# Scores of two heads issued as one stage on TensorE, and new places for the last two heads' attention product

## The reference, cut to what matters

```python
q = rms_norm(x @ q_w + q_b, nq_s).reshape(B, S, H, D)
k_img = rms_norm(img_ctx @ ki_w + ki_b, nki_s).reshape(B, -1, H, D)
v_img = (img_ctx @ vi_w + vi_b).reshape(B, -1, H, D)
scores = jnp.einsum('bshd,blhd->bhsl', q, k_img) / sqrt(D)
attn = softmax(scores)
out = jnp.einsum('bhsl,blhd->bshd', attn, v_img).reshape(B, S, INNER)
return out @ o_w + o_b
```

## Time and profile before

| | us |
|---|---|
| three runs | 1355.42, 1356.98, 1357.06 |
| median | 1356.98 |
| profiled execution: its own time | 1356.92 |
| its span | 1355.1 |
| PE busy (share of span) | 1326.7 (98%) |
| PE's weight loads busy | 1155.5 (85%) |
| DVE busy | 767.6 (57%) |
| ACT busy | 765.8 (57%) |
| POOL busy | 74.1 (5%) |

### The profile page before, as it was taken

How to read it: one execution, slowest core, us unless ns; L and a number is a source line. 1 busy time by engine, 2 the same in 40 slices (tenths; PEclk the granted TensorE clock), 3 DMA queues, 4 the chain that set the end, 5 groups by cost and what they waited for, 6 DMA issues and landing times.

```text
span 1355.1 us, 26606 instructions
## 1 busy us (share of the span) xinstructions
PE 1326.7 (98%) x10367; PEld 1155.5 (85%) x10367; DVE 767.6 (57%) x2315; ACT 765.8 (57%) x2092; POOL 74.1 (5%) x114
## 2 busy tenths in 40 slices
PE   7899999999999999999999999999999999999998
PEld 6788888988898788988889888998889888888777
DVE  7644555546555464665555465564656555554575
ACT  4375666566465574756556565556646556466522
POOL 3000000010000000000000100001000000001010
PEclk9999999999999999999999999999999999999999
DMA  8312522224122321222212231122312112122100
GB/s 303 110 63 79 141 94 68 75 63 125 48 70 64 102 94 47 63 94 79 94 47 71 70 125 63 47 79 82 110 44 79 63 63 94 48 78 65 62 1 32
DMA packets 51451, 108.47 MB, mean 80 GB/s; under 512 B 8224, under 2 KB 32000, under 8 KB 50688
## 3 DMA queue, kind: packets, MB, share of 16 engines
q1 hardware_dynamic: 51328, 106.77, 24.3%
HBM read 89.98 MB, written 16.78 MB: 79 GB/s over the span
## 4 chain that ended last, share of the span: by engine, by line
PE 86%; DVE 10%; ACT 3%; issue 1%; DMA 0%; SPq 0%; DVEq 0%
PE bank L114 57%; PE bank L1053 8%; PE bank L1063 5%; PE bank L1024 3%; PE bank L1042 3%; PE bank L1163 2%; PE bank L1175 2%; PE bank L1205 1%; PE bank L1014 1%; PE bank L1117 1%; ACT xn L785 1%; PE bank L994 1%; DVE rstd L80 1%; DVE logit L1534 1%; DVE ao_lo L1525 1%
## 5 line engine op out<-in xcount | busy, mean ns | idle before, releaser
L114 PE MATMUL bank<-sv,ct_hi 128*128 128x256 f32 x1024 | 195.7, 289 | 0.0
L114 PE MATMUL bank<-so,ao_hi 128*128 128x256 f32 x1016 | 188.2, 284 | 0.3 <-DVE ao_lo L1525 0.3
L1525 DVE SCALAR_TENSOR_TENSOR ao_lo<-bank,vecs,ao_hi 128x512 fp32r<-128x512 f32 x127 | 95.3, 751 | 159.7 <-ACT ao_hi L754 158.9
L760 ACT ACTIVATE expo<-logit,least 128x64 f32<-128x64 f32 x512 | 171.6, 337 | 20.6 <-DVE least L1536 20.6
L754 ACT ACTIVATE ao_hi<-bank,vecs 128x512 fp32r<-128x512 f32 x127 | 87.0, 685 | 155.0 <-PE bank L1053 154.5
L114 PEld LDWEIGHTS bank<-so,ao_hi 128*128 128x128 f32 x1016 | 162.4, 189 | 8.5 <-issue 0.5
L114 PEld LDWEIGHTS bank<-sv,ct_hi 128*128 128x128 f32 x1024 | 156.6, 189 | 0.1
L1534 DVE TENSOR_TENSOR logit<-bank,rr 128x256 f32<-128x256 f32 x128 | 54.4, 425 | 162.4 <-PE bank L1063 161.9
L779 ACT ACTIVATE q_sb<-bank,qbias,qscale 128x512 f32<-128x512 f32 x128 | 99.3, 776 | 80.3 <-PE bank L114 79.8
L114 PE MATMUL bank<-sv,ct_lo 128*128 128x256 f32 x512 | 143.1, 279 | 0.0
L114 PE MATMUL bank<-so,ao_lo 128*128 128x256 f32 x508 | 142.3, 280 | 0.0
(11 more groups left out here) (239 smaller groups left out, 2668.0 us busy)
## 6 DMA issues: line engine op xcount, KB each, us to landing
sv<-v_scratch SPq DMA_DIRECT2D x56, 512.0 KB, 3.4
so<-o_scratch SPq DMA_DIRECT2D x56, 512.0 KB, 3.3
xin<-in_x_dram SPq DMA_DIRECT2D x8, 512.0 KB, 4.8
cin<-in_ctx_dram SPq DMA_DIRECT2D x32, 128.0 KB, 4.8
xres<-in_x_dram SPq DMA_DIRECT2D x8, 512.0 KB, 4.7
c_scratch<-cs SPq DMA_DIRECT2D x8, 512.0 KB, 5.0
v_scratch<-sv SPq DMA_DIRECT2D x8, 512.0 KB, 3.1
o_scratch<-so SPq DMA_DIRECT2D x8, 512.0 KB, 2.6
```

Of the source, the lines that this page charges most:

```text
L114: last = pe.matmul(out, lhs[a], rhs[b], start=start and n == 0, stop=stop and n == 2, **kw)
L760: last = act.activation(expo[:, t, :], logit[:, t, :], ACT.Exp, scale=-1.0, bias=least[:, t:t + 1], accum_out=rsum[:, t:t + 1])
L1525: dve.scalar_tensor_tensor(out=lo[:, :], in0=attention_bank(g, h)[:, :], scalar=vecs[:, v:v + 1], in1=hi[:, :].bitcast(F32), op0=ALU.add, ...
```

## The change

- `OUT_LAG` goes from 4 to 3, and TensorE's step gets a new order: in even steps scores(h-2) and scores(h-1) as one stage at the head of the step; then attend(h-3), share a, K(h), share b, V(h), share c, Q(h), transposes(h-2), share d, output(h-3), share e.
- `logit`, `least`, `rsum` and `q_sb` get two buffers, and the two heads' scores go to the two halves of bank `at_ps`. `expo` is gone: the exponentials are written over `logit`. `gt` now lies in `th`.
- ACT does exps(h-2) where it did exps(h-1), behind the copy of K and share b and ahead of the copy of V. The copy of Q comes ahead of `prob_copy` in odd steps and behind it in even ones.
- DVE does both heads' logits at the head of even steps, then share a, attn_lo, share b, probabilities(h-2), share c, prob_copy(h-2).
- In the tail heads 14 and 15 each have a bank and parts of their own, and the work is put in another order; the expert choice of the group before last (`expert_choice`, `expert_scale`) comes behind the last attn_lo.

```diff
@@ -103,7 +103,7 @@
-TURN_LAG, ATT_LAG, OUT_LAG = 2, 3, 4
+TURN_LAG, ATT_LAG, OUT_LAG = 2, 3, 3
...
@@ -173,8 +173,8 @@
-    least = sb("least", [P, NT])
-    rsum = sb("rsum", [P, NT])
+    least = sb("least", [P, 2, NT])
+    rsum = sb("rsum", [P, 2, NT])
...
@@ -183,9 +183,8 @@
-    q_sb = sb("q_sb", [P, GT])
-    logit = sb("logit", [P, NT, SEQ])
-    expo = sb("expo", [P, NT, SEQ])
+    q_sb = sb("q_sb", [P, 2, GT])
+    logit = sb("logit", [P, 2, NT, SEQ])
...
@@ -249,7 +248,7 @@
-    gt = sb("gt", [E1, GT])
+    gt = th[0:E1, 0, :, :].rearrange("p c d -> p (c d)")
...
@@ -462,7 +461,7 @@
-    LAST_CHOICE_AT = {"xn3": (14, "d"), ("xt3", 0): (15, "b"), ("xt3", 1): (15, "c"), "gt": (15, "e")}
+    LAST_CHOICE_AT = {"xn3": (14, "d"), ("xt3", 0): (15, "b"), ("xt3", 1): (15, "c")}
...
@@ -486,10 +485,11 @@
-        return pj_ps[0] if (g, h) == (LAST, H - 2) else pv_ps
+        return {(LAST, H - 2): pj_ps[0], (LAST, H - 1): at_ps}.get((g, h), pv_ps)
-        return [v["k"][:, 0, 0:GT] for v in (w_hi, w_lo)] if (g, h) == (LAST, H - 2) else [ao_hi, ao_lo]
+        own = g == LAST and h >= H - 2
+        return [v["k"][:, h - (H - 2), 0:GT] for v in (w_hi, w_lo)] if own else [ao_hi, ao_lo]
...
@@ -757,12 +757,14 @@
-                last = act.activation(expo[:, t, :], logit[:, t, :], ACT.Exp, scale=-1.0, bias=least[:, t:t + 1],
-                                      accum_out=rsum[:, t:t + 1])
+                last = act.activation(logit[:, h % 2, t, :], logit[:, h % 2, t, :], ACT.Exp, scale=-1.0, bias=least[:, h % 2, t:t + 1],
+                                      accum_out=rsum[:, h % 2, t:t + 1])
+            if g == LAST and h >= H - 2:
+                act.wait_ge(pv_full.sem, pv_full.count(g, h - 1))
...
@@ -776,7 +778,7 @@
-                act.activation(q_sb[:, :], bank[:, :], ACT.Identity, scale=qscale[:, h:h + 1],
+                act.activation(q_sb[:, h % 2, :], bank[:, :], ACT.Identity, scale=qscale[:, h:h + 1],
...
@@ -882,6 +884,7 @@
+            final = main and h == H - 1 and not is_body(b, NG - 1)
...
@@ -889,19 +892,22 @@
                 project(b, h, 0)
             share(b, h, "b")
             if live(b, h - TURN_LAG):
-                prob_copy(b, h - TURN_LAG)
-            share(b, h, "c")
-            if live(b, h - 1):
-                exps(b, h - 1)
+                exps(b, h - TURN_LAG)
             if main:
                 project(b, h, 1)
-                if h == H - 1 and not is_body(b, NG - 1):
+                if final:
                     split_context(b + 1)
+            share(b, h, "c")
+            soon = main and (h % 2 == 1 or (b, h) == (LAST, H - 2))
+            if soon:
+                project(b, h, 2)
+            if live(b, h - TURN_LAG):
+                prob_copy(b, h - TURN_LAG)
+            if main and not soon:
+                project(b, h, 2)
+            if final:
+                split_tokens(b + 1)
             share(b, h, "d")
-            if main:
-                project(b, h, 2)
-                if h == H - 1 and not is_body(b, NG - 1):
-                    split_tokens(b + 1)
             share(b, h, "e")
 
         def end():
...
@@ -951,13 +957,15 @@
                 step(b, h)
         for h in range(H):
             step(LAST, h)
+        exps(LAST, H - 2)
         exps(LAST, H - 1)
+        prob_copy(LAST, H - 2)
         attn_hi(LAST, H - 3)
-        prob_copy(LAST, H - 2)
+        prob_copy(LAST, H - 1)
+        attn_hi(LAST, H - 2)
+        turned_gates(NEXT)
+        attn_hi(LAST, H - 1)
         expert_exp(NEXT)
-        attn_hi(LAST, H - 2)
-        prob_copy(LAST, H - 1)
-        attn_hi(LAST, H - 1)
         end()
 
     @block.tensor
...
@@ -1035,8 +1043,10 @@
+            elif (g, h) == (LAST, H - 1):
+                l_ready.wait(pe, g, h)
-                ao_ready.wait(pe, g, h - 2 if (g, h) == (LAST, H - 1) else h - 1)
+                ao_ready.wait(pe, g, h - 1)
...
@@ -1056,12 +1066,12 @@
-            l_ready.wait(pe, g, h - 1)
+            l_ready.wait(pe, g, h - 1 if (g, h) == (LAST, H - 1) else h - 1 - h % 2)
-                    last = pe.matmul(at_ps[i * SEQ:(i + 1) * SEQ, t * SEQ:(t + 1) * SEQ],
-                                     q_sb[:, s], k_sb[:, h % 2, keys(t, i)], start=True, stop=True)
+                    last = pe.matmul(at_ps[i * SEQ:(i + 1) * SEQ, (h % 2 * NT + t) * SEQ:(h % 2 * NT + t + 1) * SEQ],
+                                     q_sb[:, h % 2, s], k_sb[:, h % 2, keys(t, i)], start=True, stop=True)
...
@@ -1287,27 +1297,33 @@
 
         def step(b, h):
             main = live(b, h)
-            if live(b, h - OUT_LAG):
-                output(b, h - OUT_LAG)
+            if (b, h) == (0, 2):
+                gr_read.wait(pe, 0, 2 * NT - 1)
+            if h % 2 == 0 and live(b, h - 2):
+                scores(b, h - 2)
+                scores(b, h - 1)
+            if (b, h) == (LAST, H - 1):
+                scores(b, h - 1)
             if live(b, h - ATT_LAG):
                 attend(b, h - ATT_LAG)
             share(b, h, "a")
             if main and (b, h) != (0, 0):
                 project(b, h, 0)
             share(b, h, "b")
+            if main:
+                values(b, h)
+            share(b, h, "c")
             if (b, h) == (0, 1):
                 norms(-1)
-                gr_read.wait(pe, 0, 2 * NT - 1)
-            if live(b, h - 1):
-                scores(b, h - 1)
+            if main:
+                project(b, h, 2)
             if live(b, h - TURN_LAG):
                 prob_transpose(b, h - TURN_LAG)
-            share(b, h, "c")
-            if main:
-                values(b, h)
             share(b, h, "d")
-            if main:
-                project(b, h, 2)
+            if live(b, h - OUT_LAG):
+                output(b, h - OUT_LAG)
+            if (b, h) == (LAST, H - 1):
+                scores(b, h)
             share(b, h, "e")
 
         def awake(bank, n):
...
@@ -1402,16 +1418,15 @@
                 step(b, h)
         for h in range(H):
             step(LAST, h)
-        scores(LAST, H - 1)
-        gate_logits(NEXT)
-        output(LAST, H - 4)
+        turned_gates(NEXT)
+        prob_transpose(LAST, H - 2)
         attend(LAST, H - 3)
-        prob_transpose(LAST, H - 2)
+        prob_transpose(LAST, H - 1)
         attend(LAST, H - 2)
-        prob_transpose(LAST, H - 1)
         output(LAST, H - 3)
         attend(LAST, H - 1)
         output(LAST, H - 2)
+        gate_logits(NEXT)
         output(LAST, H - 1)
         end()
 
...
@@ -1516,6 +1531,8 @@
+            if g == LAST and h >= H - 2:
+                dve.wait_ge(pv_full.sem, pv_full.count(g, h - 1))
...
@@ -1528,17 +1545,20 @@
-            dve.wait_ge(qk_full.sem, qk_full.count(g, h))
+            dve.wait_ge(qk_full.sem, qk_full.count(g, h if (g, h) == (LAST, H - 2) else h + 1 - h % 2))
-            chain.link(dve.tensor_tensor(logit[:, :, :], at_ps[:, 0:NT * SEQ].rearrange("p (t l) -> p t l", t=NT),
-                                         rr[:, (g - (h < 0)) % 2, :, :], ALU.mult))
-            dve.tensor_reduce(least[:, :], logit[:, :, :], AXX, ALU.min).then_inc(l_ready.sem, 1)
+            u = h % 2
+            chain.link(dve.tensor_tensor(logit[:, u, :, :], at_ps[:, u * NT * SEQ:(u + 1) * NT * SEQ].rearrange(
+                "p (t l) -> p t l", t=NT), rr[:, (g - (h < 0)) % 2, :, :], ALU.mult))
+            dve.tensor_reduce(least[:, u, :], logit[:, u, :, :], AXX, ALU.min).then_inc(l_ready.sem, 1)
-            chain.link(dve.reciprocal(rinv[:, :], rsum[:, :]))
-            dve.tensor_tensor(prob[:, :, :], expo[:, :, :], rinv[:, :].unsqueeze(2).to_broadcast([P, NT, SEQ]),
+            if (g, h) == (LAST, H - 1):
+                dve.wait_ge(pt_full.sem, pt_full.count(g, h - 1))
+            chain.link(dve.reciprocal(rinv[:, :], rsum[:, h % 2, :]))
+            dve.tensor_tensor(prob[:, :, :], logit[:, h % 2, :, :], rinv[:, :].unsqueeze(2).to_broadcast([P, NT, SEQ]),
...
@@ -1777,23 +1797,27 @@
                     late_low(LATE_AT[at])
 
         def step(b, h):
-            if h == 0 and not is_body(b, 0) and live(b, 0):
+            first = h == 0 and not is_body(b, 0) and live(b, 0)
+            if first:
                 split(b, 0)
-            if live(b, h - TURN_LAG):
-                probabilities(b, h - TURN_LAG)
-            if h == 0 and not is_body(b, 0) and live(b, 0):
-                split(b, 1)
+            if h % 2 == 0 and live(b, h - 2):
+                logits(b, h - 2)
+                logits(b, h - 1)
+            if (b, h) == (LAST, H - 1):
+                logits(b, h - 1)
             share(b, h, "a")
             if live(b, h - ATT_LAG):
                 attn_lo(b, h - ATT_LAG)
-            if is_body(b, 0) and h == 1:
+            if first:
+                split(b, 1)
+            if (b, h) == (0, 1):
                 score_factors(0)
-            if live(b, h - 1):
-                logits(b, h - 1)
+            share(b, h, "b")
+            if live(b, h - TURN_LAG):
```

(20 more changed lines are left out.)

## The result

The changed kernel takes 1361.25 us (median of 7 runs, 1361.11 to 1361.88), the kernel before 1356.96 (7 runs, 1355.33 to 1357.20): ratio 1.0036, 95% interval 1.0025 to 1.0047. It is 4.3 us slower, where 1354.0 was predicted: the sign was wrong, the range held the time. The seven runs of the kernel before lie in two groups, three at 1355.3 to 1355.5 and four at 1357.0 to 1357.2; in the later sessions, which list the clock of each run, those near 1355.5 have a mean granted clock of 0.998 or 0.999 and the longer ones 0.997. The median and the profiled execution belong to the longer ones; against the others the change loses 5.8 us.

The account below looks back on a forecast made before the run. Only TensorE's own queue, busy 98% of the span, was taken to set the end. Terms: -15 + 5.5 + 17.8 + 7.2 - 11 - 4.5 - 2.4 - 0.4 = -2.8 us from 1356.98, giving 1354 us; range 1341 to 1366.

Parts of the forecast that it names:

- Part 3: Transposes moved into the step of their own exponentials: TensorE waits for probabilities in some steps, a loss of 17.8 us.
- Part 4: DVE's probability copy queued behind step 14's score factors: attend in step 15 waits 1.2 us in six bodies, 7.2 us lost.
- Part 2: Affinities and second attention at share b no longer run into scores: 0.8 us a body, 5.5 us lost.
- Part 5: Old waits behind DVE's scale chains and the norms' sums go away: 1.4 us, a gain of 11 us over the bodies.
- Part 1: Scores in pairs enter and leave the 64-column form once, not twice: 0.23 us for each of 64, 15 us gained.
- Parts 6 and 7: Body 0's shorter stops: at the start in step 1, gain 4.5 us; at step 14's late weights, gain 0.7 and 1.7.
- Part 8: The tail: interleaved heads 13 to 15 bring O(15) 1.0 us earlier, 0.6 given back; gain 0.4 us.
- The clock rival: Half clock follows step 14's 1.2 us stop, another 1.7 us a body, 10 us in all: 1364 us; chance 0.2.
- The first rival: The waits stay hidden: ACT's chain is ready in time, all or half the transposes' loss falls away: 1336 to 1345; chance 0.15.

Follow-up runs that it names:

- e9_halves_15: Changed kernel with tile_scales, exponentials and body 1's context low part earlier, step 14's copy ahead of share c, step 15's exponentials in halves around K's copy: 1334.62 us.
- e1_scales_early: Changed kernel with VectorE's tile_scales moved from the start of step 6 to the end of step 4: 1353.53 us.
- e4_exps_early: Changed kernel with ScalarE's exponentials earlier: ahead of the attention's high part in odd steps, two tiles ahead of K's copy in even ones: 1349.13 us.
- e8_copy_first_14: Changed kernel with VectorE's copy of the turned probabilities ahead of share c, in step 14 of bodies 1 to 7 only: 1355.72 us.
- e6_single: Changed kernel with scores no longer in pairs but one head at the head of every step: 1375.15 us.
- e3_copy_first: Changed kernel with VectorE's copy of the turned probabilities ahead of share c in every step: 1365.13 us.

## Why the prediction was wrong, by its own steps

Measured sizes come from the steps' times (first product of K to the next) of before, the changed kernel, and e9_halves_15, which has almost no waits in bodies 2 to 6.

- **Part 3, the step that failed.** It said: "3 to 10 none, as PE has 0.4 to 4 us more there". Step 6 waits 1.24 us in six bodies, and taking that away gave 7.7 us (e1_scales_early), where the distance between forecast and result is 7.2. The step compared ScalarE's chain with PE's. VectorE's chain ahead of the reciprocal was costed at step 14 and not at step 6, and nothing looked at what GpSimd does at that time. The mechanism of the rest of the part was right, and body 3 was near: there steps 0, 1 and 2 cost 0.20, 0.08 and 0.19 (0.24, 0.1, 0.2 predicted), steps 11 and 12 0.39 and 0.38 (0.37 each), step 15 0.12 to 0.20 (0.2), plain steps 0.20 (0.2). Step 14's 0.3 did not come. Where a step other than 6 waits for `prob`, the cause is ScalarE's order, as argued: e4_exps_early took these waits away. But it gave back 12.1 us for the 17.8 of the part, 1.4 in each of bodies 2 to 6 (1.8 predicted), 1.9 in body 1 (2.3), and in bodies 0 and 7 1.7 and 1.8 (3.3 and 3.2).
- **That 7.7 and 7.2 agree is partly luck.** The rest of part 3 and part 4 were taken 5.7 and 1.7 us too large, part 2 by 1.5 to 2.7; part 5 was taken too large as a gain, and the waits at body 1's start were in no part. With the sizes below, some 2 to 5 us of the result stay unassigned.
- **Part 1** (15 us): right in size, by 63 pairs and not 64, since the last two heads stay single. Two plain steps took 14.94 before and take 14.72 with no wait in e4_exps_early, 0.22 a pair where 0.23 was taken: 14 us. Scores in stages of 32 take 0.93 from first to last (0.96 predicted). Against single scores in the new place a pair is worth 0.33 to 0.36; a single there is dearer than it was behind K.
- **Part 2** (5.5 us): body 3 without waits is 160.30 less 1.44 of waits before, 158.86, and 157.90 less 0.24 in e9_halves_15, 157.66. Of this difference of 1.2 the eight pairs are 1.76 saved, which leaves 0.56 a body lost, 4 us over seven bodies, where 0.8 and 5.5 were taken. The sums of waits depend on which distance counts as undisturbed; with 1.20 and 0.16 the loss is 0.4 a body and 2.8 us. It is a remainder and wasn't tested alone.
- **Part 4** (7.2 us): right mechanism, a little large. The copy stands behind `rr` as predicted, and the wait was 0.9 us in six bodies, not 1.2; e8_copy_first_14 gave back 5.5 us.

```profile
...
634.34 2.36 DVE L1522 TENSOR_SCALAR rr<-bank,rqk 64x64 f32<-64x64 f32 x8
636.62 0.42 DVE L1536 COPY pt<-bank 64x256 f32<-64x256 f32 x1
...
```

- **Part 5** (11 us): the old waits were 1.2 to 1.44 a body in bodies 2 to 6 by the distances of starts (1.4 predicted), and none of them is left. Bodies 0, 1 and 7 had fewer, so the part is rather 8 to 9 us.
- **Parts 6 and 7** (4.5 and 2.4): step 1 of body 0 went from 9.92 to 6.69 and step 14 from 13.58 to 10.38, at full clock. Together that is 6.4 (6.9 predicted). What it missed is body 1's start, K's 1.66 us and Q's 0.51 behind the late weights; body 0 as a whole gained 5.3.
- **Part 8** (0.4): 0.9 by the table's tail.
- **Body 7** holds a small miss of its own: its step 10 cost 0.65 us, VectorE's copy behind the scale chain of share c. That is part 4's mechanism in a step not looked at.
- **The clock rival** did not come. In the changed kernel's profile the clock is full from the first body to the end of the bodies, behind step 14's stops of 0.9 us and behind step 6's of 1.24 (windows of body 3, the stop and the 3.4 us behind it). The prediction ties the half clock to the length of a stop; the last section has a stop of 2.92 us that no half clock followed.

```profile
...
549.80:551.20 1.40, 0.34 (x2) 0.00 (x0) 1.37 (x5) 0.11 (x1) 0.00 (x0) 1.00 0.00 0
551.20:554.60 3.40, 3.38 (x26) 3.39 (x27) 2.34 (x4) 1.53 (x4) 0.00 (x0) 1.00 0.06 11
...
```

The first rival, hidden waits near 1336 to 1345, is about where the same change lands once the waits are moved away by hand: 1338.41, then 1334.62.

The prediction's opening reading of PE's waits leaves out the longest of the list, 5.5 us for a DMA at the start. It is the same after (5.4), so nothing hangs on it.

## What to carry to other kernels

When operations are put ahead of others in a queue, shift that engine's whole timeline by their length and look at what the shifted work now runs beside on other engines, not only at what waits behind it. Look also at every step that has something at the letter that changed places: the same edit gave 5.5 us in step 14 of seven bodies and cost 3.9 when made in all steps. A change that saves a little everywhere and loses in three or four places is worth repairing: each wait had its own cheap move, 1361 to 1335 us.

## What the runs showed of the hardware

- Small VectorE operations stretch beside GpSimd's additions. Operations of 128x4 with two tensors from SBUF took 0.65 to 0.67 us in place of 0.16 beside additions of 128x256 (2.83 us for four, 0.71 each), and 0.16 to 0.19 beside additions of 128x2. The stretched ones start 0.70 us apart (546.61, 547.31, 548.01, 548.69), so here each lasted about as long as one addition. `ao_lo`, with one operand from a bank, took 0.75 us in both places (in e1_scales_early it ran wholly beside the additions). The Trainium skill, page "SBUF — State Buffer", section "SBUF: two separate sides", says that a VectorE operation with two SBUF inputs and a GpSimd operation that reads SBUF shut each other out for the whole instruction. The trace agrees, with these numbers.
- In the changed kernel PE stopped 1.24 us six times (1.08 of it shown as idle), and 1.66 us (1.41) at body 1's start, and the clock stayed at 2.4 GHz. Behind the stop of 2.89 us of idle in body 0 of e6_single, which ends at 59.67, it was at 1.2 GHz (0.50) for 3.4 us. But in the profiled execution of e3_copy_first it stayed at 2.4 GHz behind a stop of 2.92 us that ends at 164.56. So the length of a stop alone doesn't tell what the clock does. The four other runs of e3_copy_first, 1.7 us longer with a mean clock of 0.999, fit one half-clock stretch, which cost 1.7 us in the kernel before; they have no trace that shows it. First e6_single, then e3_copy_first, the stop and what follows (columns as in the earlier trace rows):

```profile
...
61.20:64.60 3.40, 3.40 (x15) 3.11 (x14) 1.60 (x10) 2.01 (x9) 0.00 (x0) 0.50 0.26 106
...
```

```profile
...
161.60:164.50 2.90, 0.04 (x1) 0.00 (x0) 2.69 (x9) 1.04 (x2) 0.00 (x0) 1.00 0.00 0
164.50:168.00 3.50, 3.44 (x29) 3.25 (x30) 1.86 (x9) 1.04 (x6) 0.00 (x0) 1.00 0.00 0
...
```
